# Expert update of batches 0 to 4 from stacked high and low parts, as two fp32r matmuls per tile

## The reference

```python
x_diff = x[:, None] - select_mean_diff[None, :, None, :]
x_diff = x_diff / jnp.linalg.norm(x_diff, axis=3, keepdims=True)
score = (jnp.einsum('nds,bntd->bnts', select_weight, x_diff) ** 2).sum(axis=-1)
gate = jax.nn.sigmoid(imp_slope[None, :, None] * (score - imp_center[None, :, None]))
sel_scale, sel_idx = gate.max(axis=1)[..., None], gate.argmax(axis=1)
mod_x = jnp.einsum('btdh,btd->bth', upd, x - debias)      # 8 numbers per token
degen_up = jnp.einsum('btdh,bth->btd', dgn, mod_x)
return (1.0 - sel_scale) * x + sel_scale * (bias + degen_up)
```

## Time and profile before

| | |
|---|---|
| median of 3 runs | 805.73 us (805.07 to 806.21) |
| the profiled execution: time | 805.53 us |
| its span | 803.4 us |
| granted TensorE clock, mean | 0.995 of full speed |
| busy: TensorE, DVE, ACT, POOL | 91%, 71%, 55%, 55% of the span |

### The profile page before, as it was taken

How to read it: one execution, slowest core, us unless ns; L and a number is a source line. 1 busy time by engine, 2 the same in 40 slices (tenths; PEclk the granted TensorE clock), 3 DMA queues, 4 the chain that set the end, 5 groups by cost and what they waited for, 6 DMA issues and landing times.

```text
span 803.4 us, 19513 instructions
## 1 busy us (share of the span) xinstructions
PE 735.0 (91%) x6904; PEld 670.1 (83%) x6904; DVE 573.3 (71%) x1603; ACT 445.3 (55%) x1236; POOL 438.2 (55%) x663
## 2 busy tenths in 40 slices
PE   0266788999999999999999999999999999999996
PEld 0156768999999999999989999999999998989873
DVE  7999867787775666666674565665666678888876
ACT  5734335655555657555574555555565655455422
POOL 1497866644444757544474464444384746665622
PEclk9999999999999999999999999999999999999999
DMA  9023741100010202000001020000020000000304
GB/s 215 7 56 83 170 140 34 47 8 8 7 46 8 67 8 93 12 7 7 7 25 43 1 93 8 7 7 1 8 68 7 29 8 8 7 7 21 91 12 93
DMA packets 38127, 31.59 MB, mean 39 GB/s; under 512 B 23790, under 2 KB 29294, under 8 KB 38070
## 3 DMA queue, kind: packets, MB, share of 16 engines
q1 hardware_dynamic: 37926, 30.77, 14.6%
q10 hardware_dynamic: 144, 0.07, 0.0%
HBM read 20.34 MB, written 10.49 MB: 38 GB/s over the span
## 4 chain that ended last, share of the span: by engine, by line
PE 76%; DVE 10%; POOL 6%; issue 3%; ACT 3%; DMA 0%; DVEq 0%; POOLq 0%
PE bank_quad L1509 16%; PE bank_quad L1510 16%; PE bank_quad L1511 16%; PE bank_pair L1509 4%; PE bank_pair L1510 4%; PE bank_pair L1511 4%; POOL w_lo L559 2%; PE bank_quad L1627 2%; PE bank_pair L1695 2%; PE bank L1705 1%; PE bank L1509 1%; PE bank_pair L1705 1%; PE bank L1709 1%; PE bank L1510 1%; PE bank L1511 1%
## 5 line engine op out<-in xcount | busy, mean ns | idle before, releaser
L1509 PE MATMUL bank_quad<-xt_hi,w_hi 128*128 128x256 f32 (+1 forms) x568 | 159.6, 281 | 0.0
L1510 PE MATMUL bank_quad<-xt_hi,w_lo 128*128 128x256 f32 (+1 forms) x568 | 158.9, 280 | 0.0
L1511 PE MATMUL bank_quad<-xt_lo,w_hi 128*128 128x256 f32 (+1 forms) x568 | 158.6, 279 | 0.0
L413 POOL TENSOR_TENSOR spare<-cst 1x1 f32<-1x1 f32 x86 | 17.2, 200 | 209.9 <-DVE rinv L1390 148.9
L646 POOL TENSOR_TENSOR swap<-swap,cst 128x512 f32<-128x512 f32 (+1 forms) x96 | 105.4, 1109 | 37.2 <-ACT swap L871 37.2
L928 ACT ACTIVATE sm<-sm,mx 128x128 f32<-128x128 f32 (+1 forms) x256 | 113.6, 445 | 20.3 <-DVE mx L1378 20.2
L1230 DVE TENSOR_TENSOR kq<-kq,swap 128x512 f32<-128x512 f32 (+1 forms) x96 | 90.4, 962 | 28.0 <-POOL swap L646 26.8
L1509 PEld LDWEIGHTS bank_quad<-xt_hi,w_hi 128*128 128x128 f32 x568 | 106.8, 188 | 0.0
L1510 PEld LDWEIGHTS bank_quad<-xt_hi,w_lo 128*128 128x128 f32 x568 | 106.7, 188 | 0.0
L1511 PEld LDWEIGHTS bank_quad<-xt_lo,w_hi 128*128 128x128 f32 x568 | 106.3, 187 | 0.0
L684 POOL TENSOR_SCALAR sm<-sm,rinv 128x128 f32<-128x128 f32 (+1 forms) x256 | 104.2, 420 | 0.9
(11 more groups left out here) (343 smaller groups left out, 2128.3 us busy)
## 6 DMA issues: line engine op xcount, KB each, us to landing
mixed<-st SPq DMA_DIRECT2D x32, 128.0 KB, 2.0
x<-mixed SPq DMA_DIRECT2D x32, 128.0 KB, 3.0
out<-x SPq DMA_DIRECT2D x32, 128.0 KB, 2.3
raw<-in_w_qkv SPq DMA_DIRECT2D x8, 384.0 KB, 3.7
raw<-in_w_o SPq DMA_DIRECT2D x10, 256.0 KB, 2.8
norm_mem<-in_w_qkv SPq DMA_DIRECT2D x6, 384.0 KB, 4.3
later_v<-v_next SPq DMA_DIRECT2D x16, 128.0 KB, 1.7
v_next<-later_v SPq DMA_DIRECT2D x16, 128.0 KB, 2.0
```

The source lines that it names most:

```text
L1509: mmul(dst, lh, rh, start=start and k == 0, stop=False, skip_group_check=True)
L1510: mmul(dst, ll, rh, start=False, stop=False, skip_group_check=True)
L1511: last = mmul(dst, lh, rl, start=False, stop=stop and k == n - 1, skip_group_check=True)
```

## The change

For batches 0 to 4 the 72 rows of the expert update are no longer multiplied in fp32. They are stacked into two fp32r operands of 128 rows each (`upd_m`), against two stacked forms of the weights (`upd_w`), so that two matmuls per tile give high x high, low x high and high x low. All four live in slices of `xt_lo` that belong to batches 0 and 1, which are no longer read then. Batches 5, 6 and 7 stay in fp32.

- First operand: high part of the 72 rows, and again its rows 0 to 31 in rows 96 to 127. Against it: the high part of `dw`, zeros, and the low part of `dw`'s rows 0 to 31.
- Second operand: low part of rows 0 to 63, the one-hot rows 64 to 71, and the high part's rows 32 to 63 in rows 96 to 127. Against it: high part of `dw`'s rows 0 to 63, low part of its rows 64 to 71, zeros, and low part of its rows 32 to 63.
- ScalarE: two copies of `dw` in step 1 (`update_weights`); four copies in place of one at the end of each step (`mt_stack`).
- DVE: zeroing of 32 x 1024 in step 1 (`pad_update`); the low part of the weights in three pieces in step 2 (`split_update`); the low part of the rows (`mt_rest`) behind the masks of steps 3 to 6 and of the last step.
- TensorE: `stacked_tile` in place of `update_tile`, with a wait for `mt_lo`.

```diff
         xt_l = sb("xt_lo", [P, NB, KC, S], F32R)
+        upd_w = [xt_l[:, 0, 2 * k:2 * k + 2, :].rearrange("p k s -> p (k s)") for k in range(2)]
+        upd_m = [xt_l[:, 1, k, :] for k in range(2)]
         woh = sb("wo_hi", [P, QH, D], F32R)
...
         xn_scaled, xn_added, x7_added = sem("xn_scaled"), sem("xn_added"), sem("last_xn_added")
+        upd_pad, upd_hi, upd_lo, mt_lo = sem("upd_pad"), sem("upd_hi_done"), sem("upd_lo_done"), sem("mt_lo_done")
         mt_ready, mt_done, d_ready, out_ready, stored = (
...
+            def update_weights():
+                act.wait_ge(ffn_in, 32)
+                act.wait_ge(upd_pad, 1)
+                nc.scalar.activation(upd_w[0][0:MC], dw[:], ACT.Copy)
+                nc.scalar.activation(upd_w[1][0:64], dw[0:64], ACT.Copy).then_inc(upd_hi, 1)
+
+            def mt_stack(bb):
+
+                act.wait_ge(mt_ready, bb + 1)
+                nc.scalar.activation(upd_m[0][0:MC], banks[7][0:MC, 0:S], ACT.Copy)
+                nc.scalar.activation(upd_m[0][96:128], banks[7][0:32, 0:S], ACT.Copy)
+                nc.scalar.activation(upd_m[1][96:128], banks[7][32:64, 0:S], ACT.Copy)
+                nc.scalar.activation(upd_m[1][64:MC], banks[7][64:MC, 0:S], ACT.Copy).then_inc(mt_done, 1)
+
             def exponents(i):
...
                 keep_next_v(*after)
+                if g == NG - 1 and at == 1:
+                    update_weights()
                 round_attn(i)
...
                 if needs_ffn(g, at):
-                    mt_evac(b - 2)
+                    mt_stack(b - 2)
...
+            def pad_update():
+
+                old = xt_h[64:96, 0].rearrange("p k s -> p (k s)").bitcast(F32)
+                v.tensor_tensor(xt_l[64:96, 0].rearrange("p k s -> p (k s)"), old, old, ALU.subtract).then_inc(upd_pad, 1)
+
+            def split_update(k):
+
+                if k == 0:
+                    dve.wait_ge(upd_hi, 1)
+                w, dst, src = ((0, slice(96, 128), slice(0, 32)), (1, slice(96, 128), slice(32, 64)),
+                               (1, slice(64, MC), slice(64, MC)))[k]
+                v.tensor_tensor(upd_w[w][dst], dw[src], upd_w[0][src].bitcast(F32), ALU.subtract).then_inc(upd_lo, 1)
+
+            def mt_rest(bb):
+
+                dve.wait_ge(mt_done, bb + 1)
+                v.tensor_tensor(upd_m[1][0:64], banks[7][0:64, 0:S], upd_m[0][0:64].bitcast(F32), ALU.subtract).then_inc(mt_lo, 1)
+
             def step(g, b, at):
...
                 masked_scores(i, v_group=g)
+                if needs_finish(g, at):
+                    mt_rest(b - 3)
                 if needs_norm1(g, at):
...
                 reciprocals(i)
+                if g == NG - 1 and at == 1:
+                    pad_update()
+                if g == NG - 1 and at == 2:
+                    split_update(0)
                 rope(i + 1, 0, key_bank(*step_after(g, b, at)))
                 rope(i + 1, 1)
+                if g == NG - 1 and at == 2:
+                    split_update(1)
                 if needs_finish(g, at):
...
                 rope_add(i + 1, 1)
+                if g == NG - 1 and at == 2:
+                    split_update(2)
                 rope(i + 1, 2)
...
             masked_scores(last)
+            mt_rest(NB - 4)
             reciprocals(last, (0,))
...
+            def stacked_tile(t, bank):
+
+                rows = slice(t * P, (t + 1) * P)
+                mmul(banks[bank][:], upd_m[0][:, rows], upd_w[0], start=True, stop=False)
+                mmul(banks[bank][:], upd_m[1][:, rows], upd_w[1], start=False, stop=True).then_inc(d_ready, 1)
+
+            def stacked_product(bb):
+
+                pe.wait_ge(mt_done, bb + 1)
+                pe.wait_ge(mt_lo, bb + 1)
+                for t in range(TT):
+                    stacked_tile(t, 5 + t)
+
             def update_product(bb):
...
                         pe.wait_ge(s_masked, i * 4 + 4)
-                        update_product(b - 3)
+                        if at == 3:
+                            pe.wait_ge(upd_lo, 3)
+                        stacked_product(b - 3)
                     if needs_ffn(g, at) and at > 2:
...
             pe.wait_ge(mt_done, NB - 3)
+            pe.wait_ge(mt_lo, NB - 3)
             transpose_probs(last)
...
             pe.wait_ge(f_read, NB - 2)
-            update_tile(mt[:, 0:P], 2)
+            stacked_tile(0, 2)
             pe.wait_ge(xt_hi, 2 * (2 * NB - 1))
...
                 last_part.then_inc(xt_ready, 1)
-            update_tile(mt[:, P:2 * P], 7)
+            stacked_tile(1, 7)
             for t in range(TT):
...
                 last_part = gate_tile(t, 1)
```

## The result

| | before | changed |
|---|---|---|
| median, us | 805.61 (805.07 to 806.56, 6 runs) | 812.46 (811.11 to 813.42, 6 runs) |
| ratio | | 1.0082, interval 1.0072 to 1.0093 |
| profiled span, us | 803.4 | 810.9 |

The account below looks back on a forecast made before the run. In the last group the prediction took DVE, not TensorE, to be the bound. Its terms +0.61, +0.34, +0.63, +2.0, +0.34 and -0.40 gave +3.5 us on 805.53, so 809.1; range 804.9 to 810.6.

Parts of the forecast that it names:

- Zeroing, costed at 0: Step 1, DVE: zeroing 32 x 1024 falls where DVE waits for TensorE, so 0; without cover 1.2 us.
- First two weight pieces: Step 2, DVE: both fall into waits for ScalarE's swaps, taken as 0; bound 0.9 us if the second delays a sum.
- Rival 4: Second piece loses its turn in step 2 (+0.9), or last adds meet POOL's subtraction (+1.0): 810 to 811; chance 0.1.
- Third weight piece +0.61: Step 2, DVE: the 8 x 512 piece stands between the rope sums on the chain and adds 0.61 us.
- Turned order 4 x 0.5: Steps 3 to 6: POOL's third sine product reaches the shared port before DVE's add, 0.5 us later per step, +2.0.
- low part 3 x 0.21: Steps 4 to 6, DVE: subtraction for the rows' low part ahead of the normalisation adds 0.21 us each, +0.63.
- TensorE's gain: Steps 3 to 6: two fp32 tiles, 1.72 us, become four fp32r matmuls, 1.01 us, saving 0.71 us per step.
- cover of 0.13: Steps 4 to 6: slack of 0.13 us between DVE's normalisation and TensorE's transposes, taken off the low part's 0.34.
- The same in step 3, +0.84: Step 3: low part of the rows at its full 0.34 us, and turned port order at 0.5 us.
- Low part in the tail +0.34: Tail, DVE: the low-part subtraction between masks and reciprocal lies on the chain and adds 0.34 us.
- The tile in the tail -0.40: Tail: the one expert tile on the chain gets faster on TensorE and saves 0.40 us.
- rival 2: TensorE is the bound, steps 3 to 6 each give 0.71 us and the kernel is faster: 803.2 us; chance 0.1.

Follow-up runs that it names:

- e1_pad_only: The kernel before with only the zeroing of 32 x 1024 on VectorE in step 1 added: 806.89 us, ratio 1.0013.
- e2_pieces_only: The kernel before with only ScalarE's two weight copies and VectorE's three weight pieces added: 808.25 us, ratio 1.0031.
- e3: The change with each tile again one fp32 matmul, its work on ScalarE and VectorE kept: 810.46 us, ratio 1.0063.
- e4: The change without VectorE's zeroing, weight pieces and low part of the rows; stacked tiles and ScalarE's copies kept: 807.68 us, ratio 1.0024.
- e5: The change with VectorE's third cosine product ahead of its second rotation sum in steps 3 to 6: 809.86 us, ratio 1.0062.
- e6: The change with the low part of the rows behind the reciprocals in steps 3 to 6, and later in the tail: 810.90 us, ratio 1.008.
- e9_warm: The change with two throwaway matmuls in TensorE's queue ahead of the products of step 2: 813.29 us, ratio 1.0088.
- e8: The change with cosine product before rotation sum, low part of rows later, zeroing on ScalarE and weight pieces on GpSimd: 804.28 us, ratio 0.9987.
- e11: The change without zeroing, weight pieces and low part of rows, with third cosine product before second rotation sum in steps 3 to 6: 804.31 us, ratio 0.9983.
- e12_tail_add: e8 with GpSimd's second residual sum of batch 5 in the tail held until VectorE's last gate scores are done: 804.36 us, ratio 0.9987.

## Why the prediction was wrong in size

The direction and the mechanism of steps 4 to 6 were right. The step that failed is the pricing of DVE's added work in steps 1 and 2: the zeroing and the first two weight pieces were put at nothing because they fall where DVE waits. The runs showed 1.5 us for the zeroing and 2.06 us for the pieces, 0.61 of which was forecast. Step by step, by the terms of the sum:

- *Zeroing, costed at 0*: it was **1.5 us** (e1_pad_only). "Both fall where their engine waits for TensorE" looked only at DVE's own time. DVE did wait; but the instruction had two SBUF inputs and overlapped with GpSimd's normalisation. Before, the chain of step 1 was TensorE's alone; in the change it runs through that normalisation (2.59 and 1.60 us) and DVE's sums behind it. The prediction weighed no part of the exclusion for it. Even its outer bound of 1.2 was too low.
- *First two weight pieces, the second with "I take 0, since DVE is queued first"*: DVE was not first; GpSimd's product had begun at 655.02, the piece at 655.72. The upper bound of 0.9 was the likely value, and together they measured 1.08. The first piece has a part in it that the prediction did not weigh: it made GpSimd's normalisation 0.41 longer and its first products 0.43 later. Rival 4 held this mechanism at a chance of 0.1.
- *Third weight piece +0.61*: 0.83 where it stands, and 0.43 more since the last sum, so delayed, met GpSimd's subtraction (in rival 4 too, at 0.25). Step 2 all told +2.05 (2.06 in e2_pieces_only) instead of +0.61.
- *Turned order 4 x 0.5, low part 3 x 0.21*: in steps 4 to 6 the forecast gave 22.94 + 0.71 = 23.65, measured 23.68. The mechanism was right (e3, e4 and e5 each move it alone), but that the sum is met to 0.03 is in part luck: the order with the tiles is 0.39 and not 0.5 (e4), the low part 0.35 and not 0.21 (e4 against the change; 0.31 of it comes back in e6), and TensorE's gain 0.55 and not 0.71. The cover of 0.13 was gone, it seems because DVE was by then the bound.
- *The same in step 3, +0.84*: measured +0.30, because the order was not turned there. The forecast took step 3 for the same sign as the others, with TensorE on time; in the profiled execution TensorE came late out of step 2 through the fallen clock. In e9_warm, where the clock stays at 1.00, the step is +0.88: there the term is right, and the 0.54 that the change was spared in its profile is chance.
- *Low part in the tail +0.34*: 0.2 to 0.4 (e6), about right. *The tile in the tail -0.40*: about -0.06 (e4: 39.86 against 39.92). The gate product did start earlier, and the square of the last gates then waited for GpSimd's sums. The chain of the earlier trace rows had TensorE on it, but GpSimd's sum ran 0.17 us beyond the square's start, a tie that the prediction did not look for.

By term, measured less forecast: 1.51 + 1.44 - 0.54 + 0.07 + 0.52 = 3.0 us, which is what 6.5 lies over 3.5; the third term, step 3, is that of an execution with the fall. The page of the Trainium skill on which the turned order rested, SBUF — State Buffer, section "Who interferes with whom", speaks of any DVE instruction with two SBUF inputs. The error was to apply it at one place. Every instruction that the change adds on DVE between 631 and 664 us was of that kind.

Of rival 2, that TensorE is the bound and the kernel gets faster, one half was right: in steps 4 to 6 of the kernel before TensorE was busy all of 22.94, and a kernel in which DVE keeps out of its way does get faster (e8, e11), by 0.44 a step and not 0.71.

## What to carry over

Before costing an added instruction at nothing because its engine idles there, ask which shared resource it takes and who is using it: here an instruction with two SBUF inputs in an idle gap of VectorE cost its whole length and more, while one that reads PSUM ran at its usual length under the same work of GpSimd (e5_rope_order). Where two engines reach such a resource close behind each other (here DVE led by 0.47 to 0.67 us before, and GpSimd by 0.03 to 0.10 with the faster tiles), a speed-up ahead of one of them can turn the order and make the kernel slower, and a slow-down can make it faster; so a gain on the engine that bounds the kernel has to be followed to the first tie behind it. The remedy is cheap: put the instruction that does not need the resource where the other engine would hold it.

## What the runs showed of the hardware

- The exclusion works both ways and for GpSimd's `tensor_scalar` as well: four of them took 2.61 us under the zeroing and 2.04 under the first piece (POOL 651.25 in the changed kernel), 1.62 and 1.63 before.
- A DVE `tensor_scalar` with a single SBUF input waits too: 0.68 us in e12_tail_add, 0.17 where GpSimd is idle (L1370 of e8_all_three). The kernel before has it as well: in step 2 L1338, 16 columns, took 0.43 and ended 0.04 after GpSimd's subtraction; with the change GpSimd was through by then, and it took 0.16. The Trainium skill, SBUF — State Buffer, section "Who interferes with whom", says that `tensor_scalar` can run in a two-port mode that contends with GpSimd; the trace agrees, and does not show which mode was taken. The instruction just before it, with one input in PSUM and one in SBUF, took its usual 0.75 under the same sum.
- The same wait can be followed by a fall of TensorE's granted clock in one execution and not in another. Behind waits of 2.28 us (the change) and 2.33 (e2_pieces_only) it read 0.50 to 0.65 over stretches of 2 us, for some 4 us; behind waits of 2.22 to 2.25 in e3, e5 and e6, in the same code, it read 1.00, as it did behind the 1.30 of step 1. In a part of the program that is the same in all runs, from 140 to 144 us, it read 0.57 in e1, e2 and e5 and 1.00 in the kernel before and the change. In the profile of the change, where DVE was the bound, the fall cost nothing and saved 0.58; in that of e2, where TensorE was the bound, step 3 was 0.84 longer behind it.
